# Waits on GpSimd's gather queue in the first edge attention of a four-layer graph network

## The chip, the cores and the metric

The kernel runs on one core of a Trainium2 chip. The metric is the device time of one execution in microseconds. A core has TensorE (PE), VectorE (DVE), ScalarE (ACT), GpSimd (POOL) and SyncE (SP), each with its own instruction stream; they meet only at semaphores. DMA is issued from SP, ACT or POOL.

## The reference, cut to what matters

A graph of 3125 nodes with 256 features and 103125 edges (`src`, `dst`, sorted by `dst`) goes through four layers, each normalised, rectified and added to its input. The first and the fourth are attention over edges:

```
q_att = einsum(q, relation_att)           # layer 0: one projected query and value per relation
score = sum(q_att[etype, dst] * k[src], -1) * pri / sqrt(64)       # 4 heads of 64
m     = segment_max(score, dst)
ex    = exp(score - m[dst])
agg   = segment_sum(ex / segment_sum(ex, dst)[dst] * v[src], dst)
```

Layer 1 is a node-wise attention, layer 2 a graph convolution with a mixture of 64 experts, layer 3 an attention like layer 0 with relation vectors added to the keys.

## The kernel before, in words

`attention_items` is built twice, as stage `l0e` (first edge attention, `first` is true) and `l3e` (second). The edges are packed into NI = 228 items of G = 4 groups of 128 edges; BI = 4 items make a block, and there are NBT = 57 blocks. An item holds edges of one window of 128 nodes. All loops are unrolled and the order on each engine is written out by hand.

POOL's whole work in the loop is to gather. For each item it issues four indirect DMAs (line 772), each of which fetches 128 rows of keys and values into `kv`, which has SK = 10 slots. Before item n it waits until ACT (`vwa_ready`) and DVE (`vwd_ready`) have weighed item n-10. So it comes in bursts: as soon as a block gets its weights, four slots fall free one behind the other.

For item n, TensorE turns stored queries into one query row per edge (`queries`, L958, counted in `qe_ps`), DVE multiplies with the keys (L819) and sums each head (L824, `sc_ready`). For a block m the softmax needs the maximum over all edges of a node. The path is:

- TensorE turns the block's scores (`turn_scores`, L972, `s_ps`), DVE takes a running maximum along the edges (L830) and keeps it at the ends of runs of one node (L836);
- TensorE turns these ends back (L978, L979, `fl_ps`), ACT copies them (L1057), and `spread` (L986, L988) puts them to their nodes, `m_ps`;
- DVE makes from them the nodes' maxima (L840 to L852, `mx_ready`), TensorE spreads these to the edges (`shift`, L996, `sh_ps`), and DVE subtracts them from the scores (`shifted`, L867, tile `z`);
- ACT makes the weights (`weights`, L1067), then ACT (L1049, three of four groups) and DVE (L874, L875) weigh the values, TensorE sums them per node (`sums`, L1006, `a_ps`), and DVE adds the sums to a running accumulator (`rescale` L883, `merge` L890).

DVE's order in one step t is candidates, rescale, node_max, products, run_max, drop (L857), merge, run_ends, shifted, scores, one-hots (L795 for the edges as rows, L804 turned), weigh. With t = 4m+j, block m's scores are turned at j = 0 and shifted at j = 1; the products of item t+4, the merge of item t-3 and the weighing of item t-1 stand in the same step. SP loads queries four items ahead and stores the accumulators.

Of the kernel before, what the change touches and what calls it, by code (L numbers as in the profile page):

```python
# [20 lines left out]
BI = 4  # L21
# [617 lines left out]
def attention_items(nc, name, table, ridx, q, agg, T, K, rel=None):  # L639

    with Stage(nc, name) as S:
        SK = 10
        VS = 3
        first = rel is None
# [36 lines left out]
        s_ps, run_done, fl_ready, fl_ps, flT_ready, m_ps = (S.sem(k) for k in ("s_ps", "run_done", "fl_ready", "fl_ps", "flT_ready", "m_ps"))  # L681
        cand_done, ch_done, mx_ready, d1_done, df_ready = (S.sem(k) for k in ("cand_done", "ch_done", "mx_ready", "d1_done", "df_ready"))
        sh_ps, z_ready, fac_ready, w_ready, ohf_ready = (S.sem(k) for k in ("sh_ps", "z_ready", "fac_ready", "w_ready", "ohf_ready"))
# [71 lines left out]
        @block.gpsimd  # L755
        def _(pool):
            pool.memset(crow[:, :, 0, :], 0.0)
            pool.memset(crow[:, :, 1, :], BIG)
            pool.memset(oneb[:, :], 1.0)
            pool.memset(ch[:, :, 0:1], -BIG)  # L760
            pool.memset(acc[:, BI - 1, :, :], 0.0)
            if first:
                pool.memset(K["pen"][:, :, 0:1], -BIG)
                pool.memset(K["pn"][:, :, :, 0:1], -BIG)
                pool.iota(pidi[:, :], pattern=[[0, 1]], base=0, channel_multiplier=1)
            pool.drain().then_inc(consts, 1)
            for n in range(NI):
                if n >= SK:
                    pool.wait_ge(vwa_ready, n - SK + 1)
                    pool.wait_ge(vwd_ready, n - SK + 1)  # L770
                for g in range(G):
                    pool.indirect_dma_start(kv[:, n % SK, g, :], None, table[:, :],  # L772
                                            bass.IndirectOffsetOnAxis(ap=K["recs"][:, n, g, ridx:ridx + 1], axis=0)).then_inc(kv_ready[n % SK], 16)
# [1696 lines left out]
```

## Time and profile before

| | us |
|---|---|
| median of 3 runs | 6731.64 (6724.58 to 6753.25) |
| span of the profiled execution | 6706.8 |
| first edge attention, steady stretch (block 2 to block 54) | 753.9 to 2224.6 |
| PE / DVE / ACT / POOL busy over the span | 65% / 52% / 33% / 48% |
| mean DMA rate over the span | 161 GB/s |

The profiled execution is one of its own; its span runs from the first to the last instruction, and the runs' times hold some 25 us around it. Ends of matmuls are modelled in this profile. The releaser named with a wait is inferred: names from other stages, as `l0n_skip`, and "remote" stand where no better one was found.

### The profile page before, as it was taken

To read this page: it belongs to the slowest core of one execution; us is meant where nothing else is said; L and a number is where in the kernel's file an instruction comes from. 1 tells how busy PE (TensorE), PEld (TensorE's weight loads), DVE (VectorE), ACT (ScalarE), POOL (GpSimd) and SP (SyncE) were. 2 spreads that over 40 slices of the span, in tenths; PEclk is the share of its full clock that TensorE was granted. 3 is DMA by queue.
4 is the path that set the end of the run, shared out by engine and by line. 5 is a ranking of instruction groups with operands and counts; after the bars stand their busy time and mean duration, and the time that the engine had idled before them with its cause. 6 is when DMAs were issued, how large, how long until landed. Compare 5 with 4: busy or idle time off the path is not lost. (4 is left out here: it accounts for less than half of the span.)

```text
span 6706.8 us, 90264 instructions
## 1 busy us (share of the span) xinstructions
PE 4342.6 (65%) x24913; PEld 3150.9 (47%) x24913; DVE 3458.5 (52%) x6689; ACT 2184.9 (33%) x7656; POOL 3192.9 (48%) x3187
## 2 busy tenths in 40 slices
PE   6996676766677744544444546887646666666676
PEld 4664454544445423333333435766335555555553
DVE  4452666666666662211111231112558888888885
ACT  1221455555545430000000111222225454555541
POOL 0422566666666236676676520002145565655551
PEclk8896777777777876666766778998778888888885
DMA  4334666666666525333333407882366666666673
GB/s 133 126 123 163 182 197 199 202 196 198 198 196 197 125 72 186 93 93 93 92 95 92 72 29 243 261 262 87 108 189 205 203 210 203 205 207 203 201 185 102
DMA packets 509932, 1077.03 MB, mean 161 GB/s; under 512 B 94770, under 2 KB 322388, under 8 KB 505993
## 3 DMA queue, kind: packets, MB, share of 16 engines
q0 software_dynamic: 204144, 617.42, 32.6%
q1 hardware_dynamic: 296854, 452.03, 20.2%
q10 hardware_dynamic: 8512, 2.74, 0.2%
q8 instruction: 168, 2.75, 0.2%
q14 instruction: 254, 2.08, 0.1%
HBM read 964.49 MB, written 194.54 MB: 173 GB/s over the span
## 5 line engine op out<-in xcount | busy, mean ns | idle before, releaser
L772 POOL DMA_INDIRECT l0e_kv<-t_table,k_recs x912 | 986.1, 1081 | 636.9 <-ACT l0e_vw L1049 375.5
L772 POOL DMA_INDIRECT l3e_kv<-t_table,k_recs x912 | 971.0, 1065 | 667.5 <-ACT l3e_vw L1049 368.0
L1464 PE MATMUL l2e_pA<-l2e_row,l2e_oh 128*128 128x257 f32 x1824 | 633.4, 516 | 768.7 <-issue 380.4
L1418 POOL DMA_INDIRECT l2e_row<-t_table,l2e_idx x912 | 899.7, 986 | 389.7 <-issue 265.4
L1464 PEld LDWEIGHTS l2e_pA<-l2e_row,l2e_oh 128*128 128x128 f32 x1824 | 460.0, 262 | 942.0 <-issue 852.9
L1006 PE MATMUL l0e_pA<-l0e_vw,l0e_ohf 128*128 128x260 f32 x1824 | 643.9, 500 | 198.3 <-ACT l0e_vw L1049 129.2
L958 PE MATMUL l3e_pQE<-l3e_qb,l3e_ohT 128*128 128x256 bf16 x2736 | 428.0, 318 | 405.9 <-issue 378.7
L1049 ACT ACTIVATE l3e_vw<-l3e_kv,l3e_w 128x64 f32<-128x64 f32 x2736 | 679.8, 334 | 0.0
L1049 ACT ACTIVATE l0e_vw<-l0e_kv,l0e_w 128x64 f32<-128x64 f32 x2736 | 679.6, 334 | 0.0
L1443 DVE SCALAR_TENSOR_TENSOR l2e_acc<-l2e_acc,k_itf,l2e_pA 128x257 f32<-128x257 f32 x228 | 109.9, 482 | 1058.6 <-issue 981.9
L1006 PEld LDWEIGHTS l0e_pA<-l0e_vw,l0e_ohf 128*128 128x128 f32 x1824 | 427.7, 247 | 338.5 <-ACT l0e_vw L1049 156.6
L1006 PE MATMUL l3e_pA<-l3e_vw,l3e_ohf 128*128 128x260 f32 x1824 | 534.6, 443 | 7.1 <-ACT l3e_vw L1049 6.4
L958 PE MATMUL l0e_pQE<-l0e_qb,l0e_ohT 128*128 128x256 bf16 x2736 | 451.8, 321 | 135.1 <-issue 119.1
L958 PEld LDWEIGHTS l3e_pQE<-l3e_qb,l3e_ohT 128*128 128x128 bf16 x2736 | 297.2, 112 | 509.9 <-issue 428.6
L1475 ACT ACTIVATE moe_agg<-l2e_acc 128x257 f32 x228 | 95.3, 418 | 1216.1 <-issue 658.9
L958 PEld LDWEIGHTS l0e_pQE<-l0e_qb,l0e_ohT 128*128 128x128 bf16 x2736 | 305.5, 115 | 265.5 <-issue 176.2
L1006 PEld LDWEIGHTS l3e_pA<-l3e_vw,l3e_ohf 128*128 128x128 f32 x1824 | 374.8, 217 | 77.5 <-ACT l3e_vw L1049 8.7
L814 DVE TENSOR_TENSOR l3e_kv<-l3e_kv,l3e_pD 128x1024 f32<-128x1024 f32 x228 | 276.1, 1211 | 162.0 <-remote 97.4
L1966 POOL DMA_INDIRECT comb_ya<-t_yslot,k_slot x52 | 51.8, 996 | 614.4 <-POOLq L68 593.7
L1040 ACT ACTIVATE l3e_ohf<-l3e_oh 128x512 f32<-128x512 bf16 x228 | 141.1, 619 | 493.7 <-PE l3e_pA L1006 346.3
L819 DVE TENSOR_TENSOR l0e_prod<-l0e_pQE,l0e_kv 128x1024 f32<-128x1024 f32 x228 | 276.7, 1213 | 35.2 <-remote 29.2
L819 DVE TENSOR_TENSOR l3e_prod<-l3e_pQE,l3e_kv 128x1024 f32<-128x1024 f32 x228 | 279.2, 1224 | 7.8
(469 smaller groups left out, 7126.8 us busy)
## 6 DMA issues: line engine op xcount, KB each, us to landing
exp_w<-in_L_gnn_w SPq DMA_DIRECT2D x224, 512.0 KB
t_table<-l0n_tab SPq DMA_DIRECT2D x26, 2048.0 KB, 6.9
l0e_qb<-t_q SPq DMA_DIRECT2D x228, 192.0 KB
l3e_qb<-t_q SPq DMA_DIRECT2D x228, 192.0 KB
t_agg<-l0e_acc SPq DMA_DIRECT2D x228, 130.0 KB
t_agg<-l3e_acc SPq DMA_DIRECT2D x228, 130.0 KB
l0e_drow<-t_drow SPq DMA_DIRECT2D x57, 512.0 KB
l3e_drow<-t_drow SPq DMA_DIRECT2D x57, 512.0 KB
```

Source lines behind the costliest of these rows:

```text
L772: pool.indirect_dma_start(kv[:, n % SK, g, :], None, table[:, :], bass.IndirectOffsetOnAxis(ap=K["recs"][:, n, g, ridx:ridx + 1], axis=0)) ...
L814: dve.tensor_tensor(key, key, pR.unsqueeze(2).to_broadcast([P, G, H, DK]), ALU.add).then_inc(key_done, 1)
L819: dve.tensor_tensor(prod[:, n % 2, :, :], pQE[n % 2][:, :, :], kv[:, n % SK, :, 0:D], ALU.mult).then_inc(prod_done, 1)
L958: last = pe.matmul(pQE[n % 2][:, g, :], ohT[:, m % 2, G * j + g, :], qb[:, n % QS, i, :], start=(i == 0), stop=(i == 2))
L1006: last = pe.matmul(pA[n % 2][:, 0:H * HV], ohf[:, n % 2, g, :], vw[:, v, g, :, :].rearrange("p h c -> p (h c)"), start=(g == 0), stop=(g = ...
L1040: act.activation(ohf[:, n % 2, :, :], oh[:, m % 2, G * j:G * j + G, :], ACT.Copy).then_inc(ohf_ready, 1)
L1049: last = act.activation(vw[:, v, g, h, 0:DK], kv[:, n % SK, g, D + h * DK:D + (h + 1) * DK], ACT.Copy, scale=w[:, m % 2, j, g, h:h + 1])
L1418: pool.indirect_dma_start(row[:, s, g, 0:D], None, table[:, :], bass.IndirectOffsetOnAxis(ap=idx[:, i, g:g + 1], axis=0)).then_inc(row_rea ...
L1443: dve.scalar_tensor_tensor(out=acc[:, s, :], in0=acc[:, before, :], scalar=K["itf"][:, i, 1:2], in1=pA[s % 2][:, 0:W], op0=ALU.mult, op1=A ...
L1464: last = pe.matmul(pA[s % 2][:, 0:W], oh[:, s, g, :], row[:, s, g, :], start=(g == 0), stop=(g == G - 1))
L1475: last = act.activation(all_agg[:, bass.ds(b, 1), :].rearrange("p b c -> p (b c)"), acc[:, s, :], ACT.Copy)
L1966: pool.indirect_dma_start(ya[:, t % U, k, :], None, T["yslot"][:, :], bass.IndirectOffsetOnAxis(ap=K["slot"][:, t, k:k + 1], axis=0)).then ...
```

## The change

Before the gathers of an item, POOL waits for one more semaphore in the first edge attention. Items are counted from item 2 on in bursts q of four; k is the place in the burst. The first item (k = 0) has no new wait, the second waits until the scores of block q-1 are turned, the third until its run ends are spread, the fourth until its maxima are shifted to the edges. The first burst (q = 0) and the second attention have none.

```diff
@@ -768,6 +768,9 @@
                 if n >= SK:
                     pool.wait_ge(vwa_ready, n - SK + 1)
                     pool.wait_ge(vwd_ready, n - SK + 1)
+                q, k = divmod(n - 2, BI)
+                if first and q >= 1 and k >= 1:
+                    pool.wait_ge((s_ps, m_ps, sh_ps)[k - 1], q)
                 for g in range(G):
                     pool.indirect_dma_start(kv[:, n % SK, g, :], None, table[:, :],
```

## Rows read from the trace of the kernel before

**Rows 1.** The page's head: span, and busy time of each engine.

```profile
span 6706.8 us, 90264 instructions
...
PE 4342.6 (65%) x24913; PEld 3150.9 (47%) x24913; DVE 3458.5 (52%) x6689; ACT 2184.9 (33%) x7656; POOL 3192.9 (48%) x3187
...
```

**Rows 2.** Windows view: steady stretch of the first edge attention, in one row.

```profile
...
753.90:2224.60 1470.70, 1034.93 (x6040) 730.38 (x6040) 945.69 (x1873) 744.23 (x2860) 903.68 (x832) 0.77 0.66 197
...
```

**Rows 3.** Waits view of that stretch: engine, line, releaser, total us, times, longest.

```profile
...
POOL l0e_kv L772 <- ACT l0e_vw L1049: 329.8, 53, 6.6
DVE l0e_z L867 <- remote: 257.4, 52, 7.9
...
DVE l0e_acc L890 <- issue: 137.4, 92, 4.0
...
DVE l0e_cand L840 <- DMA l0n_skip<-in_L_gnn_skip: 123.5, 51, 4.0
...
```

**Rows 4.** Timeline of block 8: start us, us, engine line op names [idle <-releaser].

```profile
...
904.92 2.28 DVE L795 TENSOR_TENSOR l0e_oh<-k_iotab,k_dlb 128x2048 bf16<-128x2048 bf16 x1
905.49 2.53 POOL L772 DMA_INDIRECT l0e_kv<-t_table,k_recs  x1 [0.31 <-issue]
...
906.26 0.27 PE L972 MATMUL l0e_pC<-k_ident,l0e_sc 128*64 128x128 f32 x1
...
910.82 0.56 PE L988 MATMUL l0e_pC<-l0e_flT,l0e_oh 128*128 128x8 bf16 x16
...
911.23 2.00 PE L1006 MATMUL l0e_pA<-l0e_vw,l0e_ohf 128*128 128x260 f32 x8
912.22 0.95 POOL L772 DMA_INDIRECT l0e_kv<-t_table,k_recs  x1 [0.30 <-issue]
...
913.94 0.23 DVE L840 COPY l0e_cand<-l0e_pC 128x64 f32<-128x64 f32 x1 [2.45 <-DMA l0n_skip<-in_L_gnn_skip]
...
915.26 0.57 PE L996 MATMUL l0e_pC<-l0e_mxb,l0e_ohT 128*128 128x4 bf16 x16 [2.03 <-issue]
...
917.47 0.94 POOL L772 DMA_INDIRECT l0e_kv<-t_table,k_recs  x1 [0.30 <-issue]
918.24 0.43 DVE L890 TENSOR_TENSOR l0e_acc<-l0e_part,l0e_pA 128x260 f32<-128x260 f32 x1 [1.82 <-issue]
...
921.22 0.95 POOL L772 DMA_INDIRECT l0e_kv<-t_table,k_recs  x1 [0.30 <-issue]
...
923.93 0.22 DVE L867 TENSOR_TENSOR l0e_z<-l0e_sc,l0e_pC 128x64 f32<-128x64 f32 x1 [5.26 <-remote]
...
928.28 1.23 POOL L772 DMA_INDIRECT l0e_kv<-t_table,k_recs  x1 [6.12 <-ACT l0e_vw L1049]
...
```

**Rows 5.** Timeline behind it, into block 9.

```profile
...
923.88 1.22 PE L958 MATMUL l0e_pQE<-l0e_qb,l0e_ohT 128*128 128x256 bf16 x5 [0.15 <-issue]
...
930.04 1.22 DVE L819 TENSOR_TENSOR l0e_prod<-l0e_pQE,l0e_kv 128x1024 f32<-128x1024 f32 x1
...
935.72 0.27 PE L972 MATMUL l0e_pC<-k_ident,l0e_sc 128*64 128x128 f32 x1
...
```

**Rows 6.** Timeline of block 55, where the gathers end.

```profile
...
2240.03 1.45 POOL L772 DMA_INDIRECT l0e_kv<-t_table,k_recs  x1 [0.30 <-issue]
...
2241.83 0.23 DVE L840 COPY l0e_cand<-l0e_pC 128x64 f32<-128x64 f32 x1 [1.17 <-PE l0e_pC L988]
...
2243.52 0.61 PE L996 MATMUL l0e_pC<-l0e_mxb,l0e_ohT 128*128 128x4 bf16 x16
...
2244.55 0.21 DVE L867 TENSOR_TENSOR l0e_z<-l0e_sc,l0e_pC 128x64 f32<-128x64 f32 x1
...
```

**Rows 7.** Timeline of one block of the second edge attention.

```profile
...
5126.47 0.56 PE L988 MATMUL l3e_pC<-l3e_flT,l3e_oh 128*128 128x8 bf16 x16
...
5127.06 0.23 DVE L840 COPY l3e_cand<-l3e_pC 128x64 f32<-128x64 f32 x1 [0.40 <-PE l3e_pC L988]
...
5128.35 0.94 POOL L772 DMA_INDIRECT l3e_kv<-t_table,k_recs  x1 [3.71 <-ACT l3e_vw L1049]
...
```

## The prediction

> **What bounds the kernel now.** First the page's head [rows 1]: no engine is busy over 65% of the span, so waits decide. The change touches one stage only, the first edge attention (tiles l0e_...). Its steady stretch, from the shift subtraction of block 2 to that of block 54, is one row of the windows view [rows 2]: 1470.70 us for 52 blocks of four items, 28.28 us a block. In it DVE is busy 945.69/52 = 18.2 us a block, ACT 14.3, POOL 17.4, the DMA engines 66%. Nothing is full.
>
> Then the waits of that stretch [rows 3]. DVE stands still before three lines: L867 (z, waits for `sh_ps`) 257.4 us, L890 (merge, waits for `a_ps` and for the store) 137.4, L840 (candidates, waits for `m_ps`) 123.5. Together 518.3/52 = 10.0 us a block, and 18.2 + 10.0 = 28.2, all but 0.1 of the period: DVE's program order is the loop that sets the period, and all three waits are mostly waits for TensorE. POOL stands idle 329.8/52 = 6.3 us a block until ACT has weighed an item; that is what starts its burst.
>
> Then one block in order of time [rows 4]. POOL's burst is 16 gathers (four items of four) nearly back to back, from about 900.0 (a period before the next one's 928.28) to 922.17. TensorE's work for DVE is done early in it: the spread (L988) ends at 911.38, but DVE's L840 starts at 913.94, 2.6 us later; the shift (L996) ends at 915.83, but L867 starts at 923.93, 8.1 us later, "remote", with DVE empty for 5.26 us. What releases it is not in the rows; what happens just before is: POOL's last gather ends at 922.17, 1.76 us earlier. TensorE's increments seem to be held while POOL writes gathers unbroken, the later in the burst the longer. Early in the burst nothing is held: the turned scores (L972) end at 906.53 in the fifth gather, and TensorE goes on from them to the end of the spread in 4.85 us with DVE's and ACT's work between.
>
> Two places where POOL is quiet say the same. In block 55 the gathers run out: the last (2240.03) ends at 2241.48, and L840 starts at 2241.83, 0.35 us later; shift and z then follow with no hold, 2244.13 to 2244.55 [rows 6]. In the second attention, same code, POOL rests 3.71 us in the middle of its burst (5124.64 to 5128.35), and L840 starts there 0.03 us after the end of L988 (5127.03 to 5127.06) [rows 7].
>
> **The change part by part.** It adds waits alone: 3 in each of 56 bursts, on POOL's queue. Behind each stand only the later gathers (POOL has no other work in this loop). A wait that is met costs nothing I can see: the vwa/vwd waits in front of the gathers leave the usual 0.30 us between gathers [rows 4].
>
> *Second item waits for the turned scores (`s_ps`).* The gathers from 905.49 to 911.92 (0.30 before 912.22) would start after 906.53, when L972 ends: about 1.1 us later. But the gather at 905.49 took 2.53 us instead of 0.95, while DVE's L795 ran from 904.92 to 907.20 [rows 4]. Started late, it loses less of this. Bounds: from -1.6 us (the stretch goes) to +1.1 us; I take zero, the gathers then ending near 911.9 as now. The Trainium skill (SBUF — State Buffer, "Who interferes with whom") states that a DVE instruction with two SBUF inputs blocks a GpSimd one that reads SBUF, until it ends. By that rule the wait is free; the row agrees with it, since the gather ends 0.8 us after L795.
>
> *Third item waits for the spread run ends (`m_ps`), fourth for the shift (`sh_ps`).* Each stops POOL right after four gathers, so the held increment comes a time r after the last of them. Bounds of r: 0.35 us (block 55, after eight gathers) and 1.76 us (after sixteen) [rows 4, 6]. The new runs before these pauses are of four or eight gathers, nearer to block 55; I take 0.75.
>
> *Do late gathers hurt?* The last item of the burst (917.47 to 922.17) is multiplied only in the second step of the next block, after its L840 (913.94 + 28.28 = 942.2). Even 5 us later it has over 10 us to land. So no consumer is on the path.
>
> *The new period, from z to z.* All numbers from [rows 4, 5]:
> - z (923.93) to the end of the next turning of scores (935.72 + 0.27): 12.06 us.
> - second item: 0.30 + 4.70 (four gathers, as 917.47 to 922.17) = 5.00. In parallel the spread ends 911.38 - 906.53 = 4.85 after the turning, so it is there when the gathers end.
> - r = 0.75, then L840 starts, and POOL its third item: 5.00. In parallel the shift ends 915.83 - 913.94 = 1.89 after L840, inside the second of these gathers.
> - r = 0.75 again, then the merge L890 (0.43) if `a_ps` was held too (it starts only at 918.24 now, though the sums end before), then z.
>
> 12.06 + 5.00 + 0.75 + 5.00 + 0.75 + 0.43 = 23.99 us, against 28.28: 4.29 us less a block. Against the present block: z comes earlier, ACT weighs earlier (z to the start of the next burst is 928.28 - 923.93 = 4.35 us), and the fourth item takes 5.00 us from z on, so the next burst follows it directly: POOL's 6.3 us of rest at the end becomes the pauses inside. Two items back to back end at z + 10.0, before the 12.06 at which `s_ps` comes, so POOL doesn't set the period. DVE at 18.2 of 24.0 has room, DMA at 0.66 x 28.28/24.0 = 78% too.
>
> Held blocks are 2 to 54 (53 of them). 53 x 4.29 = 227 us. Nothing after this stage changes, as an all-engine barrier ends it. Profiled execution: 6706.8 - 227 = 6479.8 of span; around the span the median of 6731.64 has 24.8 us more; so about 6505 us. With r at its ends: 23.19 us a block (270 us, 6462) and 26.01 us (120 us, 6611). That is this case's own range.
>
> **The rivals.**
> - *Not held at all.* With pauses, the shift ends in the sixth gather after the rest before the second item, and [rows 4] show nothing held in the fifth. Then z follows L840 by 2.72 us (2241.83 to 2244.55 [rows 6]) and not by a whole item: 12.06 + 5.00 + 0.75 + 2.72 = 20.5, but POOL's 16 gathers at 1.25 are 20.0, with the pause some 21. 53 x 7.3 = 386 us: 6346 us. Against it: POOL is then without rest again, which is the state that holds the increments; at best some blocks are so. Chance 0.12.
> - *Partly held.* Releases slower than 1.76, because the gathers' data are still landing, or because DMA at some 80% makes query loads late. 26.0 to 27.5 us a block: 6611 to 6690. Chance 0.09.
> - *No change: the hold is not POOL's.* If TensorE's increments were late for a reason of its own (8.1 us after the shift whatever POOL does), z would stay at 923.93, the fourth item would start there, end at 928.9, and the next burst at 928.9 instead of 928.28; its second item waits for `s_ps` anyway, DVE's loop is untouched: 28.3 us a block, 6732 us. Against it stand block 55 and the second attention. For it: the Trainium skill (SBUF — State Buffer, "Who interferes with whom") says that a DMA never contends with a compute engine. By that rule traffic can't hold TensorE, and only the writing of gathers by POOL is left. Chance 0.10.
> - *Slower: the hold moves to the query products.* Now POOL rests 6.12 us before a burst [rows 4], and so TensorE's increments between z and the turning are prompt. After the change the fourth item and the next first item are eight gathers without a rest, right behind z. TensorE ends the query products of the next item at 925.10, 1.2 us after z; DVE needs them at 930.04, 6.1 after z [rows 5]. If they are held from the first gather to the end of the eight (10.0 + 1.76 = 11.8), DVE waits 5.7 us there, and the period is 23.99 + 5.7 = 29.7: 53 x 1.4 = 75 us slower, 6807 us. It decides for slower once that wait exceeds 4.3 us. Against it: nothing is held in the first five gathers of today's burst, and these increments come in the first one. Chance 0.09.
>
> **How the numbers follow.** My forecast 0.60, the others as given. Time 6505 us, of the likeliest. The range 6390 to 6690 holds the forecast, the partly held, and blocks that are partly of the first rival; it leaves out the rest, about 2 in 10. What a measurement can tell here from no change is about 0.5%, 34 us: faster by more than that 0.81, within it 0.10, slower 0.09.
>
> **What would show it.** In the profile after: L867's wait "remote" falls from 257.4 us in some 52 waits to under 100; L840's and L890's fall too; POOL's largest idle is no longer for ACT's l0e_vw but for TensorE and the pauses stand between items; the steady stretch is about 1250 us for 52 blocks at some 230 GB/s; gathers that take over 2.5 us go. The second attention has the same times as before. Wrong if L867 still starts some 8 us after L996's end, or if L819 gets a wait of several us in each block: then one of the last two rivals is true.

## The result, and the profile after

The changed kernel is slower: median 6877.26 us against 6731.0 (4 runs each), ratio 1.021 with a 95% interval of 1.0182 to 1.0239. The profiled execution took 6879.54 us, its span is 6877.9. Forecast were 6505 us, in a range of 6390 to 6690.

First the page's head of the changed kernel (compare [rows 1]): all busy times are as before within 3%, so it is again a matter of waits.

```profile
span 6877.9 us, 90264 instructions
...
PE 4232.3 (62%) x24913; PEld 3121.1 (45%) x24913; DVE 3460.2 (50%) x6689; ACT 2190.2 (32%) x7656; POOL 3097.1 (45%) x3187
...
```

The windows view of its steady stretch, from z of block 2 to z of block 54 (compare [rows 2]); columns: stretch, length, busy time of PE, PEld, DVE, ACT, POOL, granted clock, DMA share, GB/s:

```profile
...
737.04:2335.80 1598.76, 941.32 (x6052) 703.93 (x6050) 947.52 (x1873) 748.30 (x2860) 823.03 (x835) 0.77 0.62 182
...
```

That is 30.75 us a block instead of 28.28: 52 x 2.47 = 128 us of the 171 that the two spans differ. Most of the rest lies in the second attention, whose code is unchanged. From its first to its last instruction it took about 1686 us before, 1720 in the changed kernel's trace, and 1721 in the trace of an experiment that wasn't slower. That part is spread between executions.

Where DVE and POOL wait in this stretch (compare [rows 3]; lines are 3 higher now, so L870 is z, L822 the products, L893 the merge, L843 the candidates, L775 the gathers and L975 the turned scores):

```profile
...
POOL l0e_kv L775 <- PE l0e_pC L975: 293.1, 30, 11.7
...
DVE l0e_prod L822 <- remote: 258.0, 45, 10.7
DVE l0e_acc L893 <- remote: 207.2, 47, 7.3
DVE l0e_cand L843 <- DMA l0n_skip<-in_L_gnn_skip: 101.2, 44, 4.0
...
DVE l0e_z L870 <- remote: 17.4, 9, 2.5
...
```

One wait was exchanged for others. The wait for the shift, 257.4 us before, is 17.4. The products (L822) waited 0.9 us before and now wait 258.0, and the merge 207.2 + 24.8 instead of 137.4. POOL's largest rest is now behind the first item of a burst, where it waits for the turned scores. One block shows how (timeline of the changed kernel, block 36 of 57):

```profile
...
1780.92 0.94 POOL L775 DMA_INDIRECT l0e_kv<-t_table,k_recs  x1 [1.50 <-PE l0e_pC L991]
...
1782.49 0.61 PE L999 MATMUL l0e_pC<-l0e_mxb,l0e_ohT 128*128 128x4 bf16 x16
...
1782.97 2.34 PE L961 MATMUL l0e_pQE<-l0e_qb,l0e_ohT 128*128 128x256 bf16 x12
...
1784.46 0.22 DVE L870 TENSOR_TENSOR l0e_z<-l0e_sc,l0e_pC 128x64 f32<-128x64 f32 x1 [1.24 <-PE l0e_pC L999]
...
1785.92 1.20 POOL L775 DMA_INDIRECT l0e_kv<-t_table,k_recs  x1 [0.30 <-issue]
...
1791.18 0.95 POOL L775 DMA_INDIRECT l0e_kv<-t_table,k_recs  x1 [0.30 <-issue]
...
1794.53 1.22 DVE L822 TENSOR_TENSOR l0e_prod<-l0e_pQE,l0e_kv 128x1024 f32<-128x1024 f32 x1 [7.89 <-remote]
...
1794.93 0.95 POOL L775 DMA_INDIRECT l0e_kv<-t_table,k_recs  x1 [0.30 <-issue]
...
1798.13 0.43 DVE L893 TENSOR_TENSOR l0e_acc<-l0e_part,l0e_pA 128x260 f32<-128x260 f32 x1 [2.38 <-remote]
...
```

The third item's gathers start at 1780.92 after their pause. The shift ends at 1783.10, in the second of them, and z follows at 1784.46, 1.4 us later (8.1 before, [rows 4]). Over all blocks, from the trace's semaphore events against the modelled end of the last matmul before each, the shift's increment is 8.05 us late at the median before and 0.86 after, the spread's 2.54 and 2.09. Lags given below as medians are read in the same way. For the query products and the sums such a reading is less sure, since of 228 increments each 54 and 57 left no event in the changed kernel's trace; of those on record 24 and 39 are over 5 us late. DVE's waits in the view above don't depend on these events.

In block 36 `sh_ps` is there before the fourth item is reached, which starts at 1785.92 with the usual 0.30 us between. Over the steady blocks the fourth item starts so in 43 of 50, and the first item of a burst in all 51. By then ACT has the weights and has begun to weigh, and the next burst's first item, which has no new wait, follows at 1791.18, again after 0.30. Twelve gathers run unbroken from 1780.92 to 1795.88, and z stands near their beginning. The query products for the next item are ready at 1785.31, but DVE starts on them at 1794.53, 9.2 us later, and the merge comes 2.25 us after the last gather.

### The profile page after: what moved, and what is told of

Read it like the earlier page. It is cut to its first block and busy times, and to the rows that moved or that the text cites. A ratio compares the mean times of both kernels' runs of the same rounds, so it can differ in the third digit from the quotient of the medians.

```text
span 6877.9 us, 90264 instructions
## 1 busy us (share of the span) xinstructions
PE 4232.3 (62%) x24913; PEld 3121.1 (45%) x24913; DVE 3460.2 (50%) x6689; ACT 2190.2 (32%) x7656; POOL 3097.1 (45%) x3187
## 3 DMA queue, kind: packets, MB, share of 16 engines
q10 hardware_dynamic: 8512, 2.74, 0.2%
## 5 line engine op out<-in xcount | busy, mean ns | idle before, releaser
L775 POOL DMA_INDIRECT l0e_kv<-t_table,k_recs x912 | 901.9, 989 | 851.6 <-PE l0e_pC L975 330.8
L775 POOL DMA_INDIRECT l3e_kv<-t_table,k_recs x912 | 966.5, 1060 | 707.0 <-ACT l3e_vw L1052 385.3
L1467 PE MATMUL l2e_pA<-l2e_row,l2e_oh 128*128 128x257 f32 x1824 | 606.7, 499 | 813.8 <-issue 395.4
L1467 PEld LDWEIGHTS l2e_pA<-l2e_row,l2e_oh 128*128 128x128 f32 x1824 | 446.2, 253 | 973.9 <-issue 889.1
L961 PE MATMUL l0e_pQE<-l0e_qb,l0e_ohT 128*128 128x256 bf16 x2736 | 430.0, 320 | 437.5 <-DVE l0e_ohT L807 395.9
L1009 PE MATMUL l0e_pA<-l0e_vw,l0e_ohf 128*128 128x260 f32 x1824 | 571.4, 463 | 70.8 <-issue 61.0
L1009 PE MATMUL l3e_pA<-l3e_vw,l3e_ohf 128*128 128x260 f32 x1824 | 551.4, 454 | 6.8 <-ACT l3e_vw L1052 6.8
L1009 PEld LDWEIGHTS l0e_pA<-l0e_vw,l0e_ohf 128*128 128x128 f32 x1824 | 404.8, 234 | 165.7 <-issue 82.0
L822 DVE TENSOR_TENSOR l0e_prod<-l0e_pQE,l0e_kv 128x1024 f32<-128x1024 f32 x228 | 276.9, 1214 | 320.8 <-remote 284.8
L1043 ACT ACTIVATE l0e_ohf<-l0e_oh 128x512 f32<-128x512 bf16 x228 | 141.7, 621 | 530.4 <-remote 482.8
```

What stands on the lines that cost most here:

```text
L822: dve.tensor_tensor(prod[:, n % 2, :, :], pQE[n % 2][:, :, :], kv[:, n % SK, :, 0:D], ALU.mult).then_inc(prod_done, 1)
L961: last = pe.matmul(pQE[n % 2][:, g, :], ohT[:, m % 2, G * j + g, :], qb[:, n % QS, i, :], start=(i == 0), stop=(i == 2))
L1009: last = pe.matmul(pA[n % 2][:, 0:H * HV], ohf[:, n % 2, g, :], vw[:, v, g, :, :].rearrange("p h c -> p (h c)"), start=(g == 0), stop=(g = ...
L1043: act.activation(ohf[:, n % 2, :, :], oh[:, m % 2, G * j:G * j + G, :], ACT.Copy).then_inc(ohf_ready, 1)
L1467: last = pe.matmul(pA[s % 2][:, 0:W], oh[:, s, g, :], row[:, s, g, :], start=(g == 0), stop=(g == G - 1))
```

## The experiments

**The theories.** *Hold*: TensorE's increments reach DVE late while POOL issues gathers unbroken; the change only moved the longest unbroken run from before z to behind it, where more of DVE's waits lie. *Cost of a wait*: each added wait costs by itself. *Traffic*: the bytes in flight hold the increments, not POOL. All experiments touch the first attention alone. (Increment: the step by which TensorE raises a semaphore when a group of matmuls is done.)

**One wait at a time.** Each of the three alone, shown against the changed kernel. The lines are those of e1; e2 and e3 differ as the remark says:

```diff
-                if first and q >= 1 and k >= 1:
-                    pool.wait_ge((s_ps, m_ps, sh_ps)[k - 1], q)
+                if first and q >= 1 and k == 1:      # e1; k == 2, m_ps: e2; k == 3, sh_ps: e3
+                    pool.wait_ge(s_ps, q)
```

> Only the wait of the second item for the turned scores is kept. Hold theory (TensorE's increments are held while POOL issues gathers unbroken, and the changed kernel moved the unbroken run of 12 gathers to right behind z): this wait comes true while the gather that DVE's L795 stretches would run, so the run of 16 stays, z stays held some 8 us: same as before, 6731 +- 25 us. Rival (each added wait costs by itself, a third of the 146 us): 6780 us.

> Only the wait of the third item for the spread is kept. Hold theory: one rest of about 1 us after the second item is enough to let the shift's increment, which falls into the second gather after it, through; z comes 7 us early, ACT weighs early, and the third, fourth and next first item run unbroken behind z as in the changed kernel: L870's wait gone, L822 and L893 wait instead, 6850 to 6900 us. Rival (each wait costs by itself): 6780 us with L870 still waiting some 5 us a block.

> Only the wait of the fourth item for the shift is kept. Hold theory: the run before it is 12 gathers unbroken, so the spread is held 2.5 us as before and the shift until 0.35 to 1.8 us after the third item's last gather: z some 4.5 us earlier than before; behind z then 8 gathers (fourth and next first item) and, as nothing holds the second, up to 16 unbroken. A gain of z is partly given back at the products: 6650 to 6850 us, L870 waiting under 2 us a block. Rival (each wait costs by itself): 6780 us with L870 unchanged.

Measured, against 6748.88 us of before in the same job: e1 6790.0 (ratio 1.0061, 1.0041 to 1.008), e2 6861.07 (1.0173, 1.0139 to 1.0206), e3 6861.86 (1.0174, 1.0147 to 1.0202). DVE's waits in the steady stretch of e1, then e2, then e3:

```profile
...
DVE l0e_z L870 <- remote: 201.9, 46, 6.7
DVE l0e_acc L893 <- issue: 199.8, 78, 6.1
DVE l0e_cand L843 <- DMA l0n_skip<-in_L_gnn_skip: 162.5, 52, 6.0
...
```

```profile
...
DVE l0e_prod L822 <- remote: 354.9, 53, 12.0
DVE l0e_acc L893 <- remote: 187.9, 45, 8.7
...
```

```profile
...
DVE l0e_prod L822 <- remote: 353.4, 49, 10.0
DVE l0e_acc L893 <- remote: 139.2, 50, 7.3
...
```

Both waits that let the shift through early (for the spread, or for the shift itself) give nearly the whole loss alone, and with the same new wait, that of the products. The shift's increment is 1.05 us late at the median in e2 and 0.01 in e3. The wait for the scores leaves it 8.13 us late, z stays held, and the kernel is 0.6% slower. "Same" was expected, so that was a miss: the merge (199.8 us against 137.4) and the candidates (162.5 against 123.5) wait longer than z gains. Why is not shown. The losses don't add up (0.6 + 1.7 + 1.7 against 2.1), so it is not a price for each wait. e3 missed its range of 6650 to 6850 by 12 us.

**A rest behind the fourth item too.** The changed kernel with a fourth wait, for the first item of a burst, which parts the twelve:

```diff
+                if first and q >= 2 and k == 0:
+                    pool.wait_ge(qe_ps, n - 1)
```

> The changed kernel with one more wait: the first item of a burst waits until TensorE has made the query products of the item two before it (qe_ps n-1). Hold theory: POOL now rests behind the fourth item until those increments are through, so the run of 12 behind z is cut to 8 and 4, the products' wait (L825 here) falls from 5.8 us a block to under 2, and the time falls clearly below the changed kernel, to 6450 to 6650 us, below before too. Rival (the gathers are late for their products, or each added wait costs by itself): slower than the changed kernel, 6900 to 6950 us.

> All three waits and the one of the first item for the query products. With the hold: 0.998 of before again. Without it: POOL's 16 gathers take 20 of 21.9 us there and the shift's wait alone keeps POOL still some us a block: 1.005 to 1.03 of before, if POOL sets the period; 1.00 if DVE does.

Measured: 6731.8 us (0.9976, 0.9961 to 0.9991), and again in a later job 6729.96 (0.9971, 0.9959 to 0.9983). One more wait takes the loss away, so waits as such don't cost, and that theory falls. The products wait no more; but the range of 6450 to 6650 was missed, and DVE's waits in the later one say why:

```profile
...
DVE l0e_z L872 <- remote: 196.6, 53, 6.7
DVE l0e_acc L895 <- issue: 163.4, 79, 5.5
DVE l0e_cand L845 <- DMA l0n_skip<-in_L_gnn_skip: 131.1, 50, 4.0
...
```

z is held again: the shift's increment is 7.4 us late at the median. The first item of a burst now starts some 8 to 11 us after z, and the second and third follow it directly, so spread and shift fall into this run of twelve. The steady stretch is 27.7 us a block. The hold was moved back and not removed. With the hold, this is the only version of the whole work below before, by 0.2 and 0.3%.

**A wait by the products, on each item**, in place of the three:

```diff
+                if first and n >= SK:
+                    pool.wait_ge(prod_done, n - 4)
```

> The three waits are replaced by one on every item: item n waits until the products of item n-5 are done, so POOL issues four gathers a step and rests in between. Hold theory: a run is four gathers, an increment is held at most some 5 us inside it and 2 us behind its end, so each step of DVE waits a little (products, merges) and none waits 8 us: 24 to 28 us a block, 6500 to 6720 us. If the runs join up again (a step is 4.6 us of DVE work, four gathers 5.0 us), it is as the changed kernel: 6850 to 6900 us. Rival (a wait costs by itself, 4 per block instead of 3): 6900 or more.

> Paced by the products of item n-5. With the hold: short runs with rests, 0.97 to 1.0 of before; if the runs join, 1.02. Without it: 1.00.

Measured: 6063.28 us (0.9996, 0.9986 to 1.0007) in the first job, 6749.87 (0.9995, 0.9977 to 1.0013) in the last. No effect in either, where the second was expected to give 0.97 to 1.0 or 1.02. In the last job the bursts are still of 16 gathers and start with the weighing, because the products are always further ahead (POOL's largest wait in its steady stretch, 744.05 to 2216.83):

```profile
...
POOL l0e_kv L775 <- ACT l0e_vw L1052: 342.7, 52, 6.9
...
```

So this one doesn't test short runs. The times point to something else, though: the kernel before took 6065.06 us in the first of these jobs.

**With and without the hold.** In three of five jobs the kernel before and everything beside it ran some 10% faster. The expectations call this two kinds of chip. That isn't shown: the results name chip 14 for the first of these jobs, which had the hold, and chip 14 again for a later one without it. So it is known only that jobs differ, not by what. In the jobs without the hold no increment of TensorE is late: in the changed kernel, run again there, the candidates and z follow TensorE at once in the middle of an unbroken run:

> The changed kernel again, because the last four kernels met a chip on which no increment of TensorE was held (0.01 us late at the median in both attentions) and the kernel before took 6065 us instead of 6731. If this job meets such a chip too: no hold to move, and the new waits come true when POOL gets there or soon after; as POOL's 16 gathers (20 us of a 21.9 us period) bound the stage there, each pause for the spread and the shift costs: 6065 to 6110 us. If it meets a chip with the hold: 1.02 of before again, 6860 to 6900 us.

```profile
...
1308.17 2.27 DVE L798 TENSOR_TENSOR l0e_oh<-k_iotab,k_dlb 128x2048 bf16<-128x2048 bf16 x1
...
1308.52 2.74 POOL L775 DMA_INDIRECT l0e_kv<-t_table,k_recs  x1 [0.30 <-issue]
...
1315.32 0.95 POOL L775 DMA_INDIRECT l0e_kv<-t_table,k_recs  x1 [0.30 <-issue]
...
1315.60 0.59 PE L991 MATMUL l0e_pC<-l0e_flT,l0e_oh 128*128 128x8 bf16 x16
...
1316.23 0.23 DVE L843 COPY l0e_cand<-l0e_pC 128x64 f32<-128x64 f32 x1
...
1319.66 0.61 PE L999 MATMUL l0e_pC<-l0e_mxb,l0e_ohT 128*128 128x4 bf16 x16
...
1320.31 0.22 DVE L870 TENSOR_TENSOR l0e_z<-l0e_sc,l0e_pC 128x64 f32<-128x64 f32 x1
...
```

L991 ends at 1316.19 and L843 starts at 1316.23; L999 ends at 1320.27, z starts at 1320.31. (The gather of 1308.52 takes 2.74 us beside DVE's build of the one-hots; that is another effect, told of at the end.) Its steady stretch, and DVE's largest wait in it:

```profile
...
728.00:1869.50 1141.50, 847.81 (x6038) 675.01 (x6037) 948.72 (x1873) 737.53 (x2860) 887.73 (x834) 0.83 0.82 254
...
```

```profile
...
DVE l0e_prod L822 <- DMA l0e_kv<-t_table,k_recs: 111.1, 70, 3.5
...
```

21.95 us a block, with gathers of the same 0.95 us at the same 1.25 us from start to start. The whole took 6071.35 us against 6057.24 of before (1.0014, 1.0001 to 1.0027), inside the 6065 to 6110 expected: without the hold the change does nothing to speak of. So its loss of 2.1% comes with the hold.

There another engine sets the pace. POOL never rests: 884 of its 912 gathers stand in one run, and the new waits are always met. 16 gathers at 1.25 us and the 1.8 us by which one of them is stretched make 21.8 of the 21.95 us, and DVE waits for gathered data instead.

Between the two kinds of job the kernel before differs by 6731 - 6057 = 674 us. Not all of that lies in this stage. From first to last instruction the first attention took 1661 us against 1318 (the kernel before with the hold, and the one paced by the products in its first job, without it; their gathers are the same), the second attention 1686 against 1518, the graph convolution 1308 against 1177. In these three POOL gathers. The experts, where it doesn't, took 590 us in both.

The traces with the hold show one thing more. Of 3021 increments of TensorE, DVE and ACT in the first attention, between 666 and 864 left no event in each trace with the hold, and at most 17 in each without. Of those on record with the hold, 149 to 262 of TensorE's are over 1 us late in each trace, none of DVE's, and none to 35 of ACT's; without the hold none at all. So "TensorE's increments alone" rests on the events that were recorded. Whether the recording of events takes part in the hold was not tested.

**Count or bytes.** Half rows: as many gathers, half the bytes. The table is viewed as rows of half the size, and the second half of each slot, the values, stays at zero. (W is D in the first attention and 2 * D in the second; `kv` is set to zero at the start; these lines are cut here.) The row numbers stay as they were, so it isn't shown that these half rows are the right keys; the test needs only their count and size.

```diff
-                    pool.indirect_dma_start(kv[:, n % SK, g, :], None, table[:, :],
+                    pool.indirect_dma_start(kv[:, n % SK, g, 0:W], None, (table.rearrange("r (k d) -> (r k) d", k=2) if first else table)[:, :],
```

> The kernel before; in the first attention each gather fetches 128 rows of half the size (the keys; the values stay at zero and are left out), so the same number of gathers, half the bytes. If the hold hangs on POOL's issuing: L867 still starts some 8 us after the shift's end and some 5 us of DVE idle a block stay, time within 30 us of before. If it hangs on the bytes in flight: the hold falls to under 2 us, the stage to 20 to 23 us a block, 6400 to 6500 us.

> Half rows (values of the first attention left out). With the hold: POOL's issuing holds: L870 still waits some 5 us a block, 0.995 to 1.005; the bytes hold: no wait, 0.95 to 0.96. Without it: 1.00.

Without the hold it was 1.001, 1.002 and 1.0006 of before in three jobs (6071.89, 6071.29, 6071.06 us). With the hold it was 6768.59 us, 1.0032 (1.0018 to 1.0047). The row of its steady stretch and DVE's waits in it there:

```profile
...
766.97:2238.10 1471.13, 1040.29 (x6027) 725.42 (x6027) 943.75 (x1872) 743.68 (x2860) 892.99 (x832) 0.77 0.43 123
...
```

```profile
...
DVE l0e_z L870 <- remote: 216.8, 50, 5.8
DVE l0e_acc L893 <- issue: 155.8, 84, 4.7
DVE l0e_cand L843 <- DMA l0n_skip<-in_L_gnn_skip: 141.9, 50, 7.0
...
```

DMA share 0.43 instead of 0.66, 123 GB/s instead of 197, and the waits are the same (216.8 + 155.8 + 141.9 = 514.5 against 518.3 [rows 3]), 28.29 us a block as before. The shift's increment is 8.10 us late at the median. The gathers' queue moved fewer packets too (16468 instead of 27200 between 900 and 1500 us). So neither bytes nor packets set the length of the hold, and the traffic theory falls. The number of gathers is left, and with it POOL's issuing and whatever comes once for each gather, such as the events of its landing. These were not told apart.

Two further kernels ran only without the hold: two of four gathers an item (the other groups left out), and plain loads by SP in place of the gathers (which rows belong to which edge is left out). Of each, the one line that matters (cut: the rest of both edits):

```diff
-                for g in range(G):
+                for g in range(2 if first else G):        # e8, in the gathers
...
+                    sp.dma_start(kv[:, n % SK, g, :], table[r:r + P, :]).then_inc(kv_ready[n % SK], 16)    # e7, on SP
```

> The kernel before; in the first attention SP loads the same bytes as plain loads of 128 neighbouring rows into the same slots, POOL issues nothing (which rows belong to which edge is left out). If the hold is POOL's: no wait of L867 at all, the shift's end to z under 1 us. If it is the traffic's: L867 still waits several us a block. The time is not comparable by itself (query loads now queue behind these on SP): 19 to 25 us a block, 6250 to 6550 us.

> SP loads the same bytes as plain loads, POOL issues nothing in the first attention (which row belongs to which edge is left out). On a chip with the hold: POOL's issuing holds: z follows the shift within 1 us; any traffic holds: L880 waits several us a block. On a chip without it the stage was 29.8 us a block, bound by SP's queue, with no increment late.

> The kernel before; in the first attention POOL gathers only two of the four groups of an item, whole rows (the other two keep zeros and are left out): half the gathers, half the bytes. Both theories: the run is 8 gathers, done before the shift, the hold goes, about 20 to 21 us a block, 6310 to 6370 us. Against the run with half rows it tells the count from the bytes.

Half the gathers: 5924.53 us (0.9762, 0.9736 to 0.9787), and again 5933.7 (0.9791). The stretch is 19.4 us a block, near DVE's own 18.1, which fits POOL setting the pace without the hold. Plain loads: 6477.29 (1.0673) and 6477.38 (1.0661); the stretch is 29.8 us a block. DVE's largest wait is the merge's for the stores (L903, t_agg), 534.3 us in 187 waits between 800 and 2200 us of the second run. SP issues loads and stores in one order, which may be why:

```profile
...
DVE l0e_acc L903 <- DMA t_agg<-l0e_acc: 534.3, 187, 7.3
...
```

Neither says anything of the hold, as there was none in their jobs. Whether plain loads or fewer gathers are free of it was not seen. The kernel paced by the products came to 1.0017 and 1.000 of before in its two further runs without the hold.

## Why the prediction was wrong

The forecast was a sum from z to z. Here are its three parts, and what the traces give for them, in us, as means over 52 blocks:

| part | forecast | before | after |
|---|---|---|---|
| z to the end of the next turned scores | 12.06 | 11.24 | 20.39 |
| from there to the candidates (second item, r) | 5.75 | 7.16 | 6.88 |
| from there to z (third item, r, merge) | 6.18 | 9.88 | 3.47 |
| period | 23.99 | 28.28 | 30.75 |

- *DVE's order sets the period, and its three waits are for TensorE's increments*: right where there is a hold. Without it z and the candidates hardly wait (g1), and POOL's gathers set the period.
- *POOL's unbroken gathers hold them*: right as far as tested. A pause moves the hold, and halving the bytes doesn't touch it. What of the gathers does it, and why some jobs have it and others not, stays open.
- *Second item, no cost*: on its own this wait went with a loss of 0.6%.
- *"r = 0.75, then L840 starts"*: right. The candidates start 0.79 us at the median after the second item's last gather. POOL's third item starts later, 1.56 us after it, and the second item ends 5.91 us after the turned scores and not 5.00.
- *"r = 0.75 again, then the merge"*: **here the step begins that failed.** It let the fourth item wait for z. The shift's increment came 0.86 us late at the median, in the second or third gather after a pause (0.67 in the second attention of the kernel before). So the fourth wait was already met in 43 of 50 blocks. For z itself that was a gain: this part took 3.47 us and not 6.18. But the rest of POOL at z, on which the sum relied, didn't exist.
- *"z to the end of the next turning of scores: 12.06 us"*: **this is the term that it spoiled.** It was read from a block in which POOL rests 6 us behind z, and it was kept for one in which POOL goes on. It measured 20.39 us, 8.3 more. In it lie the held products and merges: DVE waits for the products 258.0 us and for the merge 207.2 in the stretch, which before had 0.9 and 137.4.
- *"Two items back to back end at z + 10.0, so POOL doesn't set the period"*: true of POOL, but what counted was the hold over these items. With the third item they made twelve unbroken, and the query products that DVE needs within 6 us of z came 9.2 us late in block 36.
- *The rival "the hold moves to the query products"*, with chance 0.09, is what happened: L822 waits as described. It was priced at 75 us, with one held place and 29.7 us a block; it is 30.75 a block, as the merge is held too, and 146 us by the medians. The argument used against it, that the first five gathers of the old burst hold nothing, was read from bursts behind 6 us of rest. The change took exactly this rest away.
- *"Around the span the median has 24.8 us more"*: not so. The changed kernel's profiled execution took 6879.54 us with a span of 6877.9, so some 2 us lie around it. The 24.8 us were spread between executions. It changes nothing in the verdict.

The general fault: of a stall whose releaser the trace doesn't show, the present place was taken as the only one that could be held. Before, the shift was the one large victim. After, the unbroken gathers lay on products and merges, of which a block has four each.

## What to carry to other kernels

A wait that throttles a noisy neighbour must be judged by where its work goes, not only by what it stops overlapping: write down the whole new order of the neighbour's runs and check every handshake under each. If the same number of gathers must be issued in a shorter period, the quiet places get fewer. And look at such a stall in a second job, at another time, before tuning around it: here the stall that the change aims at was there in some jobs and absent in others.

## What the runs showed of the hardware

- In some jobs DVE sees TensorE's increments up to some 9 us after the matmul's end (9.2 in block 36) while POOL issues indirect gathers each 1.25 us. In others it never does (0.01 us at the median for all of them, with POOL going on unbroken). The kernel before takes 6731 to 6751 us in the first and 6057 to 6070 in the second. The same chip number stands with both.
- In the jobs with the hold 666 to 864 of 3021 semaphore events of the first attention are missing from each trace, in the others at most 17. A releaser named there, or a lag, is read with that in mind.
- The number of bytes of a gather doesn't matter to the hold: 28.28 and 28.29 us a block with 197 and 123 GB/s.
- A gather started beside DVE's build of the one-hots, an instruction with two bf16 inputs in SBUF, took 2.1 to 3.1 us instead of 0.95, with and without the hold, where it started in the instruction's first microsecond (905.49, 2.53 us, in [rows 4]; 1308.52, 2.74 us, in g1). The Trainium skill (SBUF — State Buffer, "Who interferes with whom") says that a DVE instruction with two inputs in SBUF contends with a GpSimd one that reads SBUF. The traces agree, as the kernel keeps a gather's row numbers in SBUF. It is another effect than the hold, since it is there with and without it.
